# A shorter gate, written-out first and last steps, and two of a tile's eight outer products on GpSimd

## The reference

```python
# flow attention, 16 heads of 8; cumsum runs over 1024 tokens of a sequence
q, k, v = sigmoid(x@Wq+bq), sigmoid(x@Wk+bk), x@Wv+bv
sink_in  = n / sum_d((q+EPS) * (cumsum(k)+EPS));   src_out = n / sum_d((k+EPS) * (cumsum(q)+EPS))
cons_sink = sum_d((q+EPS) * (cumsum(k*src_out)+EPS)) / n
cons_src  = clip(sum_d((k+EPS) * (cumsum(q*sink_in)+EPS)) / n, -1, 1)
comp = exp(cons_src) / cumsum(exp(cons_src)) * n
kv = cumsum(k[..., d] * (v*comp)[..., m])          # an 8 x 8 matrix for each head and token
a = sum_d(q*sink_in/n * kv) * sigmoid(cons_sink)
h = layernorm(x + a@Wo+bo);  z = layernorm(h + gelu(h@W1+b1)@W2+b2);  x2 = layernorm(x + z)
# mixture of 8 experts that share wi, wo and differ by a low-rank term (rank 16)
scores = softmax(x2@gate_w.T + gate_b);  the two largest give val_sum
out = sum_e count_e*val_sum * (relu(x2@wi.T + bi + (x2@A_e.T)@B_e.T) @ wo.T + bo)
result = layernorm(x2 + out)
```

## Time and profile before

| | |
|---|---|
| median of 3 runs | 451.16 us |
| the profiled execution | 451.44 us |
| its span, first to last instruction | 449.6 us |
| busy in it: PE, DVE | 383.4 us (85%), 341.6 us (76%) |
| busy in it: POOL, ACT | 226.0 us (50%), 208.2 us (46%) |
| mean granted clock of TensorE | 0.907 |
| first scan of q, tiles 0 to 7 | 8.6, 52.1, 96.0, 141.3, 188.5, 236.5, 285.2, 332.4 us |

### The profile page before, as it was taken

The page is one execution under the profiler, slowest core; times in us unless marked ns, Lnnn a source line. Parts: engine busy times, 40 slices in busy tenths (PEclk is TensorE's granted clock), DMA queues, the critical chain, the costliest instruction groups (busy, mean ns, idle before and its releaser), DMA issues.

```text
span 449.6 us, 6354 instructions
## 1 busy us (share of the span) xinstructions
PE 383.4 (85%) x2052; PEld 277.0 (62%) x2052; DVE 341.6 (76%) x819; ACT 208.2 (46%) x375; POOL 226.0 (50%) x263
## 2 busy tenths in 40 slices
PE   4675688488998998899989999899989997897792
PEld 1454556385647873696558665777478756664542
DVE  2448965998799789979897979978997899723522
ACT  2220064247543575446663674167435743554321
POOL 1013633863486349731993359426863498442201
PEclk9556969598999899899998999989998999997897
DMA  8108002700260018000730045002700170000000
GB/s 269 76 7 204 1 0 57 178 2 1 60 176 0 1 27 215 17 1 1 169 89 1 1 111 147 1 1 54 205 1 1 29 183 1 1 24 1 0 23 23
DMA packets 19856, 26.56 MB, mean 59 GB/s; under 512 B 1648, under 2 KB 9968, under 8 KB 19824
## 3 DMA queue, kind: packets, MB, share of 16 engines
q1 hardware_dynamic: 19680, 25.96, 22.6%
q10 hardware_dynamic: 144, 0.21, 0.2%
HBM read 7.29 MB, written 2.10 MB: 21 GB/s over the span
## 4 chain that ended last, share of the span: by engine, by line
PE 38%; DVE 24%; POOL 12%; issue 11%; DMA 7%; ACT 4%; SPq 3%; POOLq 0%; DVEq 0%; ACTq 0%
POOL prod L686 7%; PE pB L332 6%; PE pY L478 5%; DVE kv L870 4%; DMA vb<-vs 4%; PE pY L413 4%; PE pO L386 4%; PE pG L403 4%; DMA xT<-x_t 3%; DVE cum_kv L876 3%; SPq L274 3%; PE pA L320 2%; DVE cum_ks L766 2%; PE pG L467 2%; POOL rstd L676 2%
## 5 line engine op out<-in xcount | busy, mean ns | idle before, releaser
L686 POOL TENSOR_TENSOR prod<-cum_kv,q_fac 128x512 f32<-128x512 f32 x64 | 93.6, 1468 | 24.0 <-DVE cum_kv L876 17.0
L386 PEld LDWEIGHTS pO<-s_wor,prod 128*128 128x128 f32 x512 | 65.8, 200 | 31.7 <-POOL prod L686 22.8
L386 PE MATMUL pO<-s_wor,prod 128*128 128x128 f32 x512 | 70.8, 288 | 15.3 <-POOL prod L686 15.1
L870 DVE TENSOR_TENSOR kv<-k,vb 128x512 f32<-128x512 f32 x64 | 55.3, 864 | 5.5 <-DMA vb<-vs 5.4
L673 POOL TENSOR_TENSOR var_eps<-mv,s_con 128x4 f32<-128x4 f32 x32 | 11.4, 357 | 91.9 <-DVE mv L890 91.9
L876 DVE TENSOR_TENSOR_SCAN cum_kv<-p_ones,cum_kv,kv 128x512 f32<-128x512 f32 x32 | 40.5, 1274 | 0.6
L636 ACT ACTIVATE relu<-pG,s_att 128x512 f32<-128x512 f32 x32 | 21.9, 686 | 38.2 <-PE pG L460 38.0
L478 PEld LDWEIGHTS pY<-s_moe,gel 128*128 128x128 f32 x256 | 36.5, 223 | 4.7 <-issue 4.7
L876 DVE TENSOR_TENSOR_SCAN cum_kv<-p_ones,kv 128x512 f32<-128x512 f32 x32 | 38.5, 1214 | 0.5
L968 DVE SCALAR_TENSOR_TENSOR gel<-pG,neg_bi,relu 128x512 f32<-128x512 f32 x32 | 23.2, 743 | 19.0 <-PE pG L467 19.0
L478 PE MATMUL pY<-s_moe,gel 128*128 128x128 f32 x256 | 37.1, 305 | 0.0
(11 more groups left out here) (135 smaller groups left out, 776.6 us busy)
## 6 DMA issues: line engine op xcount, KB each, us to landing
vb<-vs SPq DMA_DIRECT2D x64, 256.0 KB, 4.6
xT<-x_t SPq DMA_DIRECT2D x8, 256.0 KB, 4.9
xt<-x SPq DMA_DIRECT2D x8, 256.0 KB, 5.3
out<-y SPq DMA_DIRECT2D x8, 256.0 KB, 2.3
s_moe<-moe_w SPq DMA_DIRECT2D x1, 836.0 KB, 10.3
s_wor<-wo_rep SPq DMA_DIRECT2D x1, 512.0 KB, 8.2
s_ffn<-ffn_w SPq DMA_DIRECT2D x1, 512.0 KB, 8.8
s_con<-consts SPq DMA_DIRECT2D x1, 502.0 KB, 5.0
```

Of the source, the lines that this page charges most:

```text
L386: mm = pe.matmul(pO3[:, s, :], prod[:, m % 4, s * P:(s + 1) * P], s_wor[:, m, :], start=False, stop=(m == DH - 1), skip_group_check=True)
L686: pool.tensor_tensor(prod[:, m % 4, :], cum_kv[t.par][:, m, :], q_fac[t.par][:, :], ALU.mult).then_inc(prod_ready, 1)
L870: dve.tensor_tensor(kv[:, m % 3, :], k[t.par][:, :], vb[:, m, :], ALU.mult).then_inc(kv_ready, 1)
```

## The change

**Gate.** Which expert is first and second is found on the logits and their exponentials instead of on the divided probabilities: the largest logit marks the first, the exponential of a logit minus the largest is 1 for it, and so the sum of the two largest probabilities is (1 + second exponential) / sum. The chain has 13 steps; the sum of exponentials and its reciprocal stand beside it (`sum_exp`, `inverse_sum_exp`). In a middle step five gate steps and the sum stand before q_sink; between the second scans and qk step 8 and the reciprocal; between qk and the expert residual step 9 alone, where 11, 12 and 13 stood.

**Outer products.** VectorE makes m = 0 to 5, GpSimd m = 6 and 7 (`late_outer_product`), between its products. Both write the same three slots. The scans stay on VectorE.

**Ends.** TensorE has an order of its own for the first two steps (`opening`, `second_step`) and for what comes after step 7 (`closing`); ScalarE too. VectorE has one for the second step and the closing, GpSimd for the second step. In the opening TensorE fills waits with matmuls on ones whose result is not used (`keep_busy`, 14 in all), v of tile 0 goes to a bank of its own, and ScalarE loads its sigmoid table with a probe before the data is there. In the second step the FFN of tile 0 stands behind the attention of tile 1. In the closing the last tile's four expert pieces have four banks (pG0, pG1, pA, pB), its first mask is transposed into pO, and the base matmuls (`inter_base`) stand before the low-rank ones. SyncE's list is unchanged.

```diff
-GATE_STEPS = 18
+GATE_STEPS = 13
 HW = SUB * HEADS
+ON_DVE = 6
...
+        def v_bank(t):
+            return pG[0] if t.n == 0 else pA
+        def expert_bank(t, f):
+            if t.n == TILES - 1 and f >= 2:
+                return (pA, pB)[f - 2]
+            return pG[f % 2]
...
+        def u1_bank(t):
+            return pO if t.n == TILES - 1 else pM
...
+            def inter_base(t, f):
                 if f == 0:
                     pe.wait_ge(x2T_ready, t.n + 1)
-                    pe.wait_ge(u1T_ready, t.n + 1)
...
+            def keep_busy(count):
+                for _ in range(count):
+                    pe.matmul(pY[:, :], onesrow[:, 0:P], onesrow[:, :], start=True, stop=True)
+            def opening(a):
+                project_q(a); project_k(a); project_v(a)
+                keep_busy(2)
+                head_sums(a, 0, True); head_sums(a, 0, False)
+                keep_busy(2)
+                denominators_T(a, 0); denominators_T(a, 1)
+                keep_busy(3)
+                head_sums(a, 1, True); head_sums(a, 1, False)
+                keep_busy(1)
+                cumulate_e(a)
+                keep_busy(2)
+                compensation_T(a); factor_T(a)
+                constant_row()
+                project_q(a.plus(1)); project_k(a.plus(1))
+                keep_busy(4)
+                pe.wait_ge(y_free[0], 16)
+                reduce_out(a, 0)
+            def second_step(b):
+                a = b.plus(1)
+                for m in range(1, 5):
+                    reduce_out(b, m)
+                head_sums(a, 0, True); head_sums(a, 0, False); project_v(a)
+                reduce_out(b, 5)
+                denominators_T(a, 0); denominators_T(a, 1)
+                reduce_out(b, 6)
+                head_sums(a, 1, True); head_sums(a, 1, False)
+                reduce_out(b, 7)
+                cumulate_e(a); h_T(b); compensation_T(a); factor_T(a)
+                for f in range(FC):
+                    hidden(b, f)
+                for f in range(FC):
+                    ffn_out(b, f)
+                reduce_out(a, 0)
+            def closing(c):
+                d = c.plus(-1)
+                inter_base(d, 2); inter1(d, 2); expert_out(d, 0); inter_base(d, 3); inter1(d, 3); expert_out(d, 1)
+                inter2(d, 2); inter2(d, 3); expert_out(d, 2); expert_out(d, 3)
+                x2_T(c); logits(c)
+                inter_base(c, 2); inter_base(c, 3)
+                lora_in(c)
+                inter_base(c, 0); inter_base(c, 1)
+                u_T(c, True); u_T(c, False)
+                for f in range(FC):
+                    inter1(c, f)
+                inter2(c, 0); inter2(c, 1)
+                expert_out(c, 0); inter2(c, 2)
+                expert_out(c, 1); inter2(c, 3)
+                expert_out(c, 2); expert_out(c, 3)
...
+            act.wait_ge(ones_ready, 1)
+            act.activation(table_probe[:, :], onesrow[:, 0:1], ACT.Sigmoid)
             act.wait_ge(att_loaded, 16)
+            def opening(a):
+                q_out(a); k_out(a)
+                spread_denominators(a, 0); spread_denominators(a, 1); v_out(a)
+                source_exp(a); alloc_tanh(a)
+                spread_scale(a, False); spread_scale(a, True)
+                q_out(a.plus(1)); k_out(a.plus(1))
+            def second_step(b):
+                a = b.plus(1)
+                v_out(a); spread_denominators(a, 0); spread_denominators(a, 1)
+                source_exp(a); alloc_tanh(a)
+                normalise(b, 0)
+                spread_scale(a, False); spread_scale(a, True)
+                h_out(b)
+                for f in range(FC):
+                    gelu(b, f)
+                normalise(b, 1)
...
+            def late_outer_product(t, m):
+                pool.wait_ge(vb_loaded[m], 16 * (t.n + 1))
+                pool.wait_ge(cumkv_ready, DH * t.n + m - 2)
+                pool.tensor_tensor(kv[:, m % 3, :], k[t.par][:, :], vb[:, m, :], ALU.mult).then_inc(kv_late_ready, 1)
...
+            def second_step(b):
+                a = b.plus(1)
+                product(b, 1); product(b, 2)
+                late_outer_product(b, 6); product(b, 3); product(b, 4); late_outer_product(b, 7)
+                product(b, 5); product(b, 6); product(b, 7)
+                inverse_std(b, 0); e_normal(a); scaled_h(b); h_residual(b); attention_input(a)
+                shifted_x(b); inverse_std(b, 1); product(a, 0); scaled_n2(b)
...
-                if B: product(b, 3); product(b, 4); product(b, 5); product(b, 6); product(b, 7); inverse_std(b, 0)
+                if B: late_outer_product(b, 6); product(b, 3); late_outer_product(b, 7); product(b, 4); product(b, 5); product(b, 6); product(b, 7); inverse_std(b, 0)
...
-                    ins = dve.tensor_tensor(prob[:, :, :], logit[:, :, :], bc(m_log[:, :]), ALU.subtract)
+                    ins = dve.tensor_tensor(below[:, :, :], logit[:, :, :], bc(m_log[:, :]), ALU.subtract)
...
+                    ins = dve.scalar_tensor_tensor(pick[:, :, :], below[:, :, :], 0.0, prefer, ALU.is_ge, ALU.mult)
...
+                    ins = dve.scalar_tensor_tensor(ex2[:, :, :], first[:, :, :], -2.0, ex[:, :, :], ALU.mult, ALU.add)
...
             def gate_total(t):
-                dve.wait_ge(gate_step, GATE_STEPS * t.n + 13)
+                dve.wait_ge(gate_step, GATE_STEPS * t.n + 8)
...
-                dve.tensor_tensor(gate_sum[:, :], top1[:, :], top2[:, :], ALU.add).then_inc(gsum_ready, 1)
+                dve.scalar_tensor_tensor(gate_sum[:, :], top2[:, :], 1.0, r_ex[:, :], ALU.add, ALU.mult).then_inc(gsum_ready, 1)
...
+            def closing(c):
+                d = c.plus(-1)
+                second_relu(d, 2); second_relu(d, 3)
+                expert_residual(d); moments(d, 3)
+                for i in range(6):
+                    gate(c, i)
+                masked_lora(c, True)
+                for i in range(6, GATE_STEPS):
+                    gate(c, i)
+                masked_lora(c, False)
+                sum_exp(c); inverse_sum_exp(c);gate_total(c)
+                for f in range(FC):
+                    second_relu(c, f)
+                expert_residual(c); moments(c, 3)
+            def second_step(b):
+                a = b.plus(1)
...
+                outer_product(b, 4); cumulate_kv(b, 3); cumulate_kv(b, 4)
+                cumulate_q(a); cumulate_k(a); k_times_cum_q(a, 0); q_times_cum_k(a, 0)
+                outer_product(b, 5); cumulate_kv(b, 5)
+                inverse_denominators(a); normal_denominators(a)
+                cumulate_kv(b, 6)
+                sink(a); cumulate_sink(a); source(a); k_times_cum_q(a, 1); cumulate_source(a); q_times_cum_k(a, 1)
+                cumulate_kv(b, 7)
+                conserved(a); clip_source(a)
+                moments(b, 0)
+                prefix_e(a); allocation(a)
+                inverse_cum_e(a); source_factor(a); sink_factor(a)
+                values(a); query_factor(a)
+                outer_product(a, 0); cumulate_kv(a, 0); outer_product(a, 1); cumulate_kv(a, 1); outer_product(a, 2)
+                moments(b, 1)
+                outer_product(a, 3); cumulate_kv(a, 2)
+                moments(b, 2)
...
-                if B: cumulate_kv(b, 5); outer_product(b, 6); cumulate_kv(b, 6); outer_product(b, 7)
+                if B: cumulate_kv(b, 5); cumulate_kv(b, 6)
...
-            run_steps(step)
+            step(Tile(-1))
+            second_step(Tile(0))
+            run_steps(step, first=1, end=TILES)
+            closing(Tile(TILES - 1))
```

164 lines of the change are left out of this document (96 added, 68 removed).

## The result

Eight runs of the changed kernel had a median of 446.21 us (443.68 to 449.13), eight of the kernel before beside them 451.37 us. The ratio is 0.989, 95% interval 0.985 to 0.994: faster by 5.2 us, where 10.3 was forecast. The profiled execution is the fastest of the eight (443.68, span 441.9), so a part of the distance lies between the executions of this kernel: the three slowest had a mean granted clock of 0.915 or 0.916, the profiled one 0.926. Medians in this document are of all executions, while the ratios and intervals leave out those that took over 1.5% more than the fastest of the same kernel (two of the twelve of e5, one of the six of e10, one or two of the kernel before in some sets).

A forecast was written before the change was run, and what follows sets the result against it. Limits: half-clock TensorE handoffs at the start, GpSimd's last product and VectorE waiting for TensorE in the middle, one tile's serial work at the end. -2.3 + 1.6 + 0 - 0.6 + 1.1 - 10.1 = -10.3: 441 us, range 434 to 446.5.

The forecast's parts named there:

- Opening, -6.4: Tile 0 up to its values: values at 25.0 instead of 31.35 us, 6.4 us earlier.
- no gain from the clock, -2.5: Opening's lower bound: only 2.5 us gained if the dummy matmuls do not keep TensorE's clock up.
- lie in waits and cost nothing: Opening: the 14 dummies fit in waits of 1.3 to 4.4 us; each overhanging one would cost up to 0.9.
- Second step, -2.3: Tile 0's products with tile 1's attention: tile 1's values at 64.65, `res2` ending at 82.4 instead of 84.69, -2.3 us.
- Middle, 0: Steps 2 to 6, two outer products moved to GpSimd: no gain or loss, bounds -1.2 and +1.7 us each.
- VectorE decided: Rival, middle steps: shorter GpSimd tail gains up to 1.2 us each, 434 us; sign: period shorter by over 0.5; chance 0.19.
- Slower by blocked GpSimd operations: Rival: seven GpSimd operations at blocked length, 1.47 us instead of 1.23 each; +12 in seven steps, 453 us; chance 0.07.
- Gate, -0.6: Gate cut from 18 to 13 steps: -0.1 us in each of six steps, -0.6 in all.
- Step 1, +1.6: Step 1: kq, qk and products 6 and 7 take turns; head sums end near T+18.0 instead of T+16.3, +1.6 us.
- Step 7, +1.1: Step 7: without a next tile, the moments of `pO` wait directly for the last reduction, +1.1 us.
- the clock falls: Rival, closing: TensorE's clock falls as in the profile before, +5 us, 446 us; chance 0.10.
- Closing, -10.1: From tile 7's x2 transposes to the last expert residual: residual starts at 430.85 instead of 441.00, -10.1 us.

The follow-up runs named there:

- e2: Changed kernel without the 14 full-width dummy matmuls of its opening; median 447.67 us, ratio 0.989 to the kernel before.
- e13: Changed kernel with short dummy matmuls (128 columns) in TensorE's waits in the second step alone; median 445.57 us, ratio 0.987 to the kernel before.
- e3: Changed kernel with the second step in the order of before, new opening kept; median 441.50 us, ratio 0.980 to the kernel before.
- e12: Changed kernel with last tile's outer products 6 and 7 on VectorE, old second-step order, short dummies between the groups of the second head sums; median 430.55 us.
- e14: Combined version (last-tile products on VectorE, old second step, second-head-sum dummies) with outer products 6 and 7 of all tiles on VectorE; median 436.09 us.
- e1: Changed kernel with all eight outer products on VectorE again; opening, second step, gate and closing kept; median 441.28 us, ratio 0.976 to the kernel before.
- e5: Kernel before with only outer products 6 and 7 moved to GpSimd; median 456.26 us, ratio 1.008 to the kernel before.
- e8: Kernel before with the short gate alone; median 448.42 us, ratio 0.994 to the kernel before.
- e4: Kernel before with five short dummy matmuls around the last reductions and before the head sums in steps 2 to 6; median 451.73 us, ratio 0.999.
- e10: Kernel before with short dummies around the last reductions and head sums, and three more between the second head sums' groups; median 445.89 us, ratio 0.988.
- e7: Changed kernel with short dummy matmuls in step 7 alone, where TensorE waits for GpSimd's products; median 442.33 us, ratio 0.982 to the kernel before.
- e6: Changed kernel with outer products 6 and 7 of the last tile alone back on VectorE; median 441.62 us, ratio 0.976 to the kernel before.
- e9: Changed kernel with the closing alone as before (general step, two banks for expert pieces); median 455.51 us, ratio 1.010 to the kernel before.

## Why the prediction was right and wrong

- **Opening, -6.4: -5.1.** The mechanism was right but for one thing: the bound "no gain from the clock, -2.5" was off. Without any dummy the opening gives 4.4 (e2). I had booked 3.9 us to the clock; but the first head sums, ahead of which project_v now runs, kept the full clock without a dummy (1.04 in e2). And the 5.1 is partly luck: "lie in waits and cost nothing" failed in six of the ten profiled executions with the dummies, where the values come 3.3 to 3.7 us earlier than before.
- **Second step, -2.3: +0.8. Failed.** The step that failed is "followed with the row durations: 64.65 for the values of tile 1"; they came at 68.13. From the values on (16.5 forecast, 15.6 measured) it was sound. I had taken the durations of rows at full clock for a stretch in which TensorE stands idle between products: a reduction at 39.49 takes 2.08 us, not 1.06. e13 gives that 1.5 us between `q_sink` and the values, and e3 shows that the order costs 4.7 us as a whole. What in the order costs the rest stays open. (The working also has two slips: 65.2 + 3.5 + 1.9 + 0.9 + 3.6 is 75.1, and the FFN at the full clock would give -3.9.)
- **Middle, 0: right for the move, within its bounds.** At an equal clock it gives 0.2 to 0.3 us a step (e12 against e14); the sums of five steps differ by 0.5 and 0.6 (e1 and e5), in which falls of the clock weigh more than the move. Last product at T+14.3 (forecast T+14.5), head sums at T+16.2 (T+16.4), the new wait of 1.20 us. The recorded sign of "VectorE decided" did come: from `q_sink` to `q_sink` five steps went from 47.9 to 46.6 us each. It misled, since e1 has all outer products on VectorE and its middle is as short. "Slower by blocked GpSimd operations" is out as well: from 322.20 to 331.27 its seven operations take 9.07 us, a pitch of 1.30. The time of 449 by the rule of the Trainium skill (SBUF — State Buffer, section "SBUF: two separate sides"), 1.2 us more a tile, didn't come either: at an equal clock a middle step is 0.2 to 0.3 shorter with the move.
- **Gate, -0.6: mis-sized.** Steps 2 to 6 gained 4.6 in all, 2.6 of it with the gate alone (e8). At a clock of 1.00 and with all outer products on VectorE a step lasts 46.2 to 46.6 with the long gate (e4, e10, whose dummies may have a part in it; one more lasts 47.15, with its wait of 2.23 us for xT) and 45.8 to 46.0 with the short one (e1, e8, e14): some 0.4 a step instead of 0.1. The rest is how many steps fall. The step that failed here is that no term of the sum had the clock of the middle, though the earlier trace rows show the wait of 0.94 us, and the windows of before have 0.96 in every step.
- **Step 1, +1.6: +0.8**, right in kind: qk (L937) takes 1.65 us instead of 0.68, and the head sums end at T+16.9, not T+18.0. The price isn't fixed: e5 has +2.4, and e1, with the move undone, has a step 1 of 46.54 against 45.81.
- **Step 7, +1.1: +4.6. Failed.** The step that failed is that the sum charged only the later last product, and took the reductions behind it at the full clock. The later product costs 0.8 (e7 against e6); the rest, 3.8, is the half clock. The rival "the clock falls" was drawn, but for the closing alone. It was the right mechanism at the wrong place.
- **Closing, -10.1: -9.4** in the profile, at a clock of 1.00 throughout; e9 puts it at 8.0 in the profile and 9.3 between the medians. The rival's fall didn't come.
- **Sum.** The profiled execution lost 2.5 us against the forecast (+3.1 at the start, -0.8 in step 1, -4.0 in the middle, +3.5 in step 7, +0.7 at the end). So the -4.0 that no term foresaw hid more than half of the two failures, and that is luck. The median lost another 2.5. Four of the seven other executions have a lower clock (0.915 to 0.922), but two have a higher one (0.927, 0.930) and still took 446.88 and 445.54. Part of it may be the opening: e6 and e7, with the same first two steps, have `res2` of tile 0 at 85.05 and 85.60 instead of 83.77.

## What to carry to other kernels

Where TensorE is the engine that the others wait for, cut the profile into steps and put the granted clock beside each length before anything is costed: an edit may be worth little by its own microseconds and much by the gap that it opens or closes in front of TensorE. Look for the next gap at once, since filling one alone can leave the time as it was (e4, 0; e4 and the second gap, 6.4). Profile more than one execution before a single number is trusted: the same code fell in one and not in the next. Decide for each tile by itself what is handed to GpSimd: in the last tile, with no next tile's work in TensorE's queue, the same two operations that were harmless in the middle cost 4.6 us.

## What the runs showed of the hardware

- A fall of TensorE from 2.4 to 1.2 GHz in a middle step costs 0.5 to 1.9 us with the short gate (45.5 to 46.0 at a mean of 1.00, 46.5 to 47.8 at 0.96), a fall in step 7 3.8 us.
- The fall follows a short idle time, but not each one, and the length of that one wait doesn't decide: with [0.81 <-DVE qk] at 251.57 it came, with [0.76 <-DVE qk] at 299.00 in the same execution it did not; in e14 it came behind 0.41 us at 237.87 and not behind 0.82 in the next step. What decides is open.
- The scatter between executions goes with the clock in e12: its six lay between 428.4 (mean clock 0.961) and 432.9 (0.950). In the changed kernel it does so only in part (443.7 at 0.926, 445.5 at 0.930).
- A dummy matmul is no free filler: at half clock four records of 128x512 took 3.55 us instead of 1.88 to 1.96.
- A kernel can have the higher clock and not be faster: the profiled execution of e13 had 0.949 and took 443.67 us, that of the changed kernel 0.926 and 443.68. Its dummies overhang: twelve take 2.84 us, and `q_sink` of tile 1 came 1.0 later.
